# A mixture-of-experts block on one core: gathered token rows transposed by a transposing DMA instead of TensorE

## The chip, the cores and the metric

One Trainium2 chip, and one of its cores is used. The metric is the device time of one execution in microseconds (us); lower is better. The engines are called PE (TensorE, matmuls), DVE (VectorE), ACT (ScalarE), POOL (GpSimd) and SP (SyncE). SP computes nothing here; it issues DMAs.

## What is computed

The input `x` has 4 batches of 512 tokens of 512 features. Each batch first gets a sparse attention matrix added, and then a feed-forward part runs over the normalised tokens. What matters here is its routed half:

```python
logits = x @ router_w.T                         # 8 experts
topk_w, topk_idx = top_k(softmax(logits), 2)    # 2 experts a token, weights normalised to 1
for each expert e:                              # I = 352 hidden features
    out = silu(x @ gate_w[e]) * (x @ up_w[e]) @ down_w[e]
    acc = acc + combine[:, e] * out
moe = acc + shared expert(x)                    # hidden size 704, for all tokens
return x + moe
```

## The kernel before

Four batches are processed in turn (scores, thresholds, normalisation, the shared expert). All of that is the same in both kernels and ends at about 344 us. Then come the routed blocks, which the change touches.

**Blocks.** The 2048 tokens times 2 experts are sorted by expert and cut into blocks of 128 rows. There are up to 39 blocks (`BLOCKS`); 35 are in use with these inputs. For each block j the normalised rows are fetched from DRAM by an indirect DMA (the gather), multiplied by the weights of one expert, scaled by the router's weight, and added into the output in DRAM by another indirect DMA (the scatter, which accumulates). Each value is kept as two float16 parts, hi and lo, so a gathered row has 2 x 512 float16 elements, and each product takes three matmuls. Most tiles of the routed part have two buffers, and block j uses buffer j % 2. Of the gathered rows `xg` these are `qT` and `kT`, of the transposed rows `xT2` two regions of `xT`.

**The steps of block j, by engine.**

- POOL: `gather(j, p)` (lines 548 to 551) copies 128 row numbers into `gidx` (L549), waits for that copy, and issues the gather into `xg` (L550). `scatter(j, m, p)` (lines 553 to 563) waits for the block's result (`s_y2`) and for the scatter before it to have landed (`d_sc`), copies the row numbers into `sidx` (L561), and issues the scatter (L562).
- PE: `routed_x` (L1022) transposes the gathered rows by 8 transposes into bank 0 (L1030). `routed_up` (L1033) runs 24 matmuls for gate and up (L1044 to L1049). `routed_hT` (L1052) transposes the hidden features by 3 transposes (L1057). `routed_down` (L1060) runs 9 matmuls (L1068 to L1070).
- DVE: `routed_x` (L1422) copies bank 0 to `xT2` (L1427), `routed_hidden` forms the product of gate and up (L1433), `routed_h` the lo part of the hidden features (L1438).
- ACT: the activation of the gate (L798), the hi part of the hidden features (L804), and the scaled result into `y2` (L812), for which it waits until the scatter two blocks earlier has landed.

**Order.** Each engine runs its own program in order, and semaphores tie them together. PE's step j is: hidden transposes of j-1, row transposes of j+1, up j, down j-1. DVE's step j is: lo part of j-1, copy of the transposed rows of j+1, two units of expert weights, product of j. ACT's step j is: hi part of j-1, two units of weights, activation of j, result of j-1. POOL's step j waits until PE has transposed block j+1, issues the gather of block j+3 into the buffer that this frees, and then issues the scatter of block j-1. `run_blocks` (L1469) writes out the first 21 steps, loops to 33, and nests the rest in conditions on the number of blocks in use.

**Expert weights.** Each expert has 7 units: 4 of gate and up (two DMAs of 176 KB) and 3 of down (one DMA of 256 KB). SP loads them in float32 into 4 staging places (L400, in `load_ranked`, which waits until the place is free again), ACT makes the hi part (L610) and DVE the lo part (L1121). The first expert and part of the second are there before block 0, and steps 0 to 20 take two units each. SP's program before the change simply goes through the 8 experts (lines 432 to 436), so each load is issued when its place comes free.

Of the kernel before, what the change touches and what calls it, by code (L numbers as in the profile page):

```python
# [59 lines left out]
HEAD_BLOCKS = 21  # L60
GROUP = 8
# [64 lines left out]
def build(nc, x, ctx_in, wq, wk, gamma, router, gate, up, down, s_gate, s_gate_b, s_up, s_up_b, s_down, s_down_b,  # L126
# [6 lines left out]
    def sem(name):  # L133
        return es.enter_context(nc.semaphore(name))
# [72 lines left out]
    sg2 = sgt[:, :, 0:I]  # L207
    xT2 = xT[:, :, :, :].rearrange("p s c t -> p (s c t)")[:, 0:4 * KD * P].rearrange("p (a s c t) -> p a s c t", a=2, s=2, c=KD)
# [66 lines left out]
    d_xg = [sem(f"d_xg{i}") for i in range(2)]  # L275
    d_sc = [sem(f"d_sc{i}") for i in range(2)]
# [52 lines left out]
    s_x2ps = sem("s_x2ps")  # L329
    s_x2 = sem("s_x2")  # L330
# [16 lines left out]
    def _(sp):  # L347
# [85 lines left out]
        for r in range(E):  # L433
            expert = sp.value_load(order[0:1, r:r + 1].bitcast(I32), min_val=0, max_val=E - 1)
            for n in range(RANKED + r * PER_EXPERT, RANKED + (r + 1) * PER_EXPERT):
                load_ranked(n, expert)
# [6 lines left out]
    def _(pool):  # L443
# [135 lines left out]
        pool.wait_ge(s_x2ps, 1)  # L579
# [3 lines left out]
        def step(j, m, p, fetch=True):  # L583
            if fetch:
                pool.wait_ge(s_x2ps, j + 2)
                gather(j + 3, 1 - p)
            if not (isinstance(j, int) and j == 0):
                scatter(j - 1, m if p else m - 1, 1 - p)
# [244 lines left out]
    def _(pe):  # L833
# [188 lines left out]
        def routed_x(j, m, p):  # L1022
            pe.wait_ge(d_xg[p], 16 * (m + 1))
            if isinstance(j, int) and j == 0:
                pe.wait_ge(s_route, 1)
            else:
                pe.wait_ge(s_x2, j)
            o = bank[0][:, :].bitcast(F16)
            for c in range(2 * KD):
                last = pe.transpose(o[:, c * P:(c + 1) * P], xg[p][:, c * P:(c + 1) * P], ident16[:, :])  # L1030
            last.then_inc(s_x2ps, 1)

        def routed_up(j, p, at):  # L1033
            pe.wait_ge(s_x2, j + 1)
# [41 lines left out]
        def step(j, m, p, fetch=True):  # L1076
            first_block = isinstance(j, int) and j == 0
            if not first_block:
                routed_hT(j - 1, 1 - p)
            if first_block or not (isinstance(j, int) and j == BLOCKS - 1):  # L1080
                routed_x(j + 1, m + (1 if p else 0), 1 - p)
            at = where(j)
            if not isinstance(j, int):
                pe.wait_ge(s_wloD, EARLY + (E - 1) * PER_EXPERT)
            elif j == 0:
                pe.wait_ge(s_wlo, SECOND - EARLY)
            elif j % 4 == 0 and j < HEAD_BLOCKS:
                pe.wait_ge(s_wloD, EARLY + j // 4 * PER_EXPERT)
            routed_up(j, p, at)
            if not first_block:  # L1090
                routed_down(j - 1, 1 - p, where(j - 1))

        routed_x(0, 0, 0)
# [9 lines left out]
    def _(dve):  # L1103
# [318 lines left out]
        def routed_x(j, p):  # L1422

            dve.wait_ge(s_x2ps, j + 1)
            if not (isinstance(j, int) and j < 2):
                dve.wait_ge(s_gu2, j - 1)
            dve.tensor_copy(xT2[:, p, :, :, :].rearrange("p s c t -> p (s c t)").bitcast(F32), bank[0][:, :]).then_inc(s_x2, 1)  # L1427

# [12 lines left out]
        def step(j, m, p, fetch=True):  # L1441
# [3 lines left out]
            if first_block or not (isinstance(j, int) and j == BLOCKS - 1):  # L1445
                routed_x(j + 1, 1 - p)
# [6 lines left out]
        def later_weights(k):  # L1453
            for _ in range(k):
                weight_lo(next(later))

        later_weights(4)
        routed_x(0, 0)
        later_weights(sum(SECOND_AT) - 4)

# [53 lines left out]
```

## Time and profile before

| | us |
|---|---|
| median of 3 runs | 588.96 |
| lowest and highest | 588.16, 589.74 |
| the profiled execution | 589.12 |
| its span | 587.3 |
| mean granted clock of TensorE | 0.906 of full speed |

The span runs from the first to the last instruction; the time of the execution has 1.8 us more around it. In the profile, busy time is the time in which an engine ran instructions; L1030 is line 1030 of the kernel; "x34" is a count. A wait is put down to what released it. PE overlaps the end of one matmul with the next, so the time of one (mean ns) is longer than the distance of two. "SPq" is the queue of SP, in which issues of DMAs are seen. A DMA "lands" when its semaphore says that all its data have arrived; the time to landing counts from its issue.

### The profile page before, as it was taken

Reading aid. Unit: us, or ns where it says so; the run is one execution under the profiler, and the core shown is the slowest. Engines: PE = TensorE matmul, PEld = TensorE weight load, DVE = VectorE, ACT = ScalarE, POOL = GpSimd, SP = SyncE. Lnnn points to the kernel's source line nnn. Section 1 sums busy time; section 2 is a strip of 40 time slices with the busy share of each in tenths; the row PEclk is TensorE's granted clock in tenths of the full one; section 3 lists DMA queues with packets and bytes.
Section 4 is the critical chain, followed back from the end, with each engine's and each line's share of the span. In section 5 each row is a group of like instructions: output and inputs, shape, how many; then the busy total and the mean of one; then the engine's idle time right before and its main releaser. Section 6 shows DMA issues by size and latency. Waiting matters only on the chain.

```text
span 587.3 us, 9556 instructions
## 1 busy us (share of the span) xinstructions
PE 478.6 (81%) x2914; PEld 269.9 (46%) x2915; DVE 341.8 (58%) x890; ACT 236.0 (40%) x417; POOL 196.2 (33%) x247
## 2 busy tenths in 40 slices
PE   5220539979799869976898989999999999999970
PEld 2000324434343434433445546666666666666640
DVE  1699787688677976785299365545545533223210
ACT  3552265443654374443443244444444432222220
POOL 0012245004300070004219433544454454544531
PEclk9765769999699988998699799999999999999985
DMA  5701240004700162005333295677688745454451
GB/s 139 247 18 36 90 144 19 1 0 128 179 1 1 71 133 83 1 1 145 73 99 104 86 266 174 158 208 188 163 199 181 171 74 94 83 89 90 75 91 18
DMA packets 36926, 60.51 MB, mean 103 GB/s; under 512 B 6153, under 2 KB 16649, under 8 KB 36882
## 3 DMA queue, kind: packets, MB, share of 16 engines
q0 software_dynamic: 10384, 23.34, 21.9%
q1 hardware_dynamic: 26498, 36.60, 19.6%
q8 instruction: 25, 0.41, 0.3%
q14 instruction: 19, 0.16, 0.1%
HBM read 37.64 MB, written 22.28 MB: 102 GB/s over the span
## 4 chain that ended last, share of the span: by engine, by line
PE 61%; DVE 20%; ACT 6%; issue 6%; DMA 3%; POOL 3%; DVEq 0%; SPq 0%; ACTq 0%; POOLq 0%
PE bank L925 5%; PE bank L926 5%; PE bank L927 5%; PE bank L1068 4%; PE bank L1070 4%; PE bank L1069 4%; PE bank L1044 4%; PE bank L1048 3%; PE bank L1046 3%; PE bank L1047 3%; PE bank L1049 3%; PE bank L1045 3%; PE bank L1030 3%; PE bank L871 2%; PE bank L1057 2%
## 5 line engine op out<-in xcount | busy, mean ns | idle before, releaser
L925 PE MATMUL bank<-xT,W 128*128 128x512 f16 x176 | 69.8, 397 | 0.0
L926 PE MATMUL bank<-xT,W 128*128 128x512 f16 x176 | 69.8, 396 | 0.0
L927 PE MATMUL bank<-xT,W 128*128 128x512 f16 x176 | 69.5, 395 | 0.0
L562 POOL DMA_INDIRECT out_dram<-xb,sidx x35 | 56.8, 1624 | 29.7 <-POOL sidx L561 28.6
L1438 DVE TENSOR_TENSOR hS<-bank,hS 128x384 f16<-128x384 f32 x35 | 19.5, 558 | 73.4 <-ACT hS L804 67.3
L798 ACT ACTIVATE sgt<-bank 128x352 f32<-128x352 f32 x35 | 16.2, 463 | 86.2 <-PE bank L1049 86.2
L1433 DVE SCALAR_TENSOR_TENSOR xb<-bank,sgt 128x352 f32<-128x352 f32 x35 | 18.4, 525 | 54.7 <-ACT sgt L798 54.7
L492 POOL TENSOR_TENSOR rstd<-pw 128x4 f32<-128x4 f32 x12 | 12.5, 1042 | 107.4 <-DVE pw L1149 107.1
L812 ACT ACTIVATE xb<-bank,wcol 128x512 f32<-128x512 f32 x35 | 24.1, 688 | 56.8 <-PE bank L1070 55.3
L937 PE MATMUL bank<-W,hS 128*128 128x512 f16 x96 | 37.1, 387 | 10.8 <-DVE hS L1303 9.4
L1044 PE MATMUL bank<-W,xT 128*128 x140 | 43.8, 313 | 0.2 <-issue 0.2
L1046 PE MATMUL bank<-W,xT 128*128 x140 | 43.8, 313 | 0.0
L1049 PE MATMUL bank<-W,xT 128*128 x140 | 43.8, 313 | 0.0
L1047 PE MATMUL bank<-W,xT 128*128 x140 | 43.8, 313 | 0.0
L1045 PE MATMUL bank<-W,xT 128*128 x140 | 43.8, 313 | 0.0
L1048 PE MATMUL bank<-W,xT 128*128 x140 | 43.8, 313 | 0.0
L662 ACT ACTIVATE sgt<-bank,bias 128x512 f32<-128x512 f32 (+1 forms) x24 | 16.5, 687 | 66.0 <-PE bank L927 66.0
L1068 PE MATMUL bank<-W,hS 128*128 x105 | 40.5, 386 | 1.3 <-DVE hS L1438 1.3
L1069 PE MATMUL bank<-W,hS 128*128 x105 | 40.6, 386 | 0.0
L1070 PE MATMUL bank<-W,hS 128*128 x105 | 40.6, 386 | 0.0
L938 PE MATMUL bank<-W,hS 128*128 128x512 f16 x96 | 36.9, 384 | 0.0
L939 PE MATMUL bank<-W,hS 128*128 128x512 f16 x96 | 36.9, 384 | 0.0
(230 smaller groups left out, 1082.5 us busy)
## 6 DMA issues: line engine op xcount, KB each, us to landing
xn_dram<-xn SPq DMA_DIRECT2D x17, 256.0 KB, 2.0
xb<-x_in SPq DMA_DIRECT2D x4, 1024.0 KB, 6.4
out_dram<-xb SPq DMA_DIRECT2D x16, 256.0 KB, 2.6
out_dram<-ysh POOLq DMA_DIRECT2D x12, 256.0 KB, 4.1
stage<-L_ffn_down_w_in SPq DMA_DIRECT2D x12, 256.0 KB
sim<-L_ffn_down_w_in SPq DMA_DIRECT2D x12, 256.0 KB
stage<-L_ffn_gate_w_in SPq DMA_DIRECT2D x16, 176.0 KB
stage<-L_ffn_up_w_in SPq DMA_DIRECT2D x16, 176.0 KB
```

What stands on the lines that cost most here:

```text
L925: pe.matmul(o, wh, xT[:, 0, c, :], start=(c == 0), stop=False)
L926: pe.matmul(o, wh, xT[:, 1, c, :], start=False, stop=False)
L927: last = pe.matmul(o, wl, xT[:, 0, c, :], start=False, stop=(c == KD - 1))
L1044: pe.matmul(og, xh, W[:, bass.ds(hi, I)], start=f, stop=False)
L1045: pe.matmul(ou, xh, W[:, bass.ds(hi + I, I)], start=f, stop=False)
L1046: pe.matmul(og, xh, W[:, bass.ds(lo, I)], start=False, stop=False)
L1047: pe.matmul(ou, xh, W[:, bass.ds(lo + I, I)], start=False, stop=False)
L1048: pe.matmul(og, xl, W[:, bass.ds(hi, I)], start=False, stop=z)
L1049: last = pe.matmul(ou, xl, W[:, bass.ds(hi + I, I)], start=False, stop=z)
L1068: pe.matmul(o, hh, wh, start=(c == 0), stop=False)
L1069: pe.matmul(o, hh, wl, start=False, stop=False)
L1070: last = pe.matmul(o, hl, wh, start=False, stop=(c == DC - 1))
```

## The change

PE's eight transposes a block and DVE's copy go. In their place SP issues one transposing DMA a block, from `xg` to `xT2`, which turns the 128 rows of 1024 float16 elements into 8 tiles of 128 x 128. `xT2` and the new view `xt2` are the same memory. SP issues it for block j+2 in its step j, after the wait for the gather (`d_xg`) and for the up matmuls of block j (`s_gu2`), which read the same buffer. PE's up part of block j waits for the landing (`d_xt`) instead of DVE's copy. POOL's gather of block j+3 waits for the landing of the transposing DMA of block j+1 instead of PE's transposes. SP has one program for both: the loads of weights are now cut into portions, 11 units ahead of the first transposing DMA, 7 behind the second, and then two units in each of the steps 0 to 18, ahead of that step's transposing DMA.

```diff
--- before.py
+++ after.py
@@ -58,6 +58,7 @@
 BLOCKS = T * TOPK // P + E - 1
 SURE = 33
 HEAD_BLOCKS = 21
+LOADING = 19
 GROUP = 8
 TABLE_AT = {3: (0, 8), 4: (8, 16), 5: (16, 2 * NT)}
 PLACES = 4
@@ -205,6 +206,7 @@
     y2 = xb[:, 0:2, :]
     h2 = xb[:, 2:4, 0:I]
     sg2 = sgt[:, :, 0:I]
+    xt2 = xT[:, :, :, :].rearrange("p s c t -> p (s c t)")[:, 0:4 * KD * P].rearrange("p (a n t) -> p a n t", a=2, n=2 * KD)
     xT2 = xT[:, :, :, :].rearrange("p s c t -> p (s c t)")[:, 0:4 * KD * P].rearrange("p (a s c t) -> p a s c t", a=2, s=2, c=KD)
     hT2 = hS[:, :, 0:DC, 0:2 * P].rearrange("p s c (a t) -> p s c a t", a=2)
     rt = sigA[:, :, :].rearrange("p a b -> p (a b)")
@@ -273,6 +275,7 @@
     d_y = [sem(f"d_y{i}") for i in range(2)]
     d_stage = [sem(f"d_stage{i}") for i in range(PLACES)]
     d_xg = [sem(f"d_xg{i}") for i in range(2)]
+    d_xt = [sem(f"d_xt{i}") for i in range(2)]
     d_sc = [sem(f"d_sc{i}") for i in range(2)]
     s_const = sem("s_const")
     s_zero = sem("s_zero")
@@ -326,8 +329,6 @@
     s_oneh = sem("s_oneh")
     s_tabp = sem("s_tabp")
     s_route = sem("s_route")
-    s_x2ps = sem("s_x2ps")
-    s_x2 = sem("s_x2")
     s_gu2 = sem("s_gu2")
     s_sig2 = sem("s_sig2")
     s_h2 = sem("s_h2")
@@ -430,10 +431,45 @@
             if b + 1 < NB:
                 sp.dma_start(xb[:, :, :], x[b + 1].rearrange("(t p) d -> p t d", p=P)).then_inc(d_x, 16)
         sp.wait_ge(s_order, 1)
-        for r in range(E):
-            expert = sp.value_load(order[0:1, r:r + 1].bitcast(I32), min_val=0, max_val=E - 1)
-            for n in range(RANKED + r * PER_EXPERT, RANKED + (r + 1) * PER_EXPERT):
-                load_ranked(n, expert)
+        ranked = iter(range(RANKED, len(UNITS)))
+        expert = [None]
+
+        def load_more(k):
+
+            for _ in range(k):
+                n = next(ranked)
+                if (n - RANKED) % PER_EXPERT == 0:
+                    r = (n - RANKED) // PER_EXPERT
+                    expert[0] = sp.value_load(order[0:1, r:r + 1].bitcast(I32), min_val=0, max_val=E - 1)
+                load_ranked(n, expert[0])
+
+        def routed_x(j, m, p):
+
+            sp.wait_ge(d_xg[p], 16 * (m + 1))
+            if not (isinstance(j, int) and j < 2):
+                sp.wait_ge(s_gu2, j - 1)
+            sp.dma_start_transpose(xt2[:, p, :, :], xg[p][:, :]).then_inc(d_xt[p], 16)
+
+        load_more(PER_EXPERT + PLACES)
+        sp.wait_ge(s_route, 1)
+        sp.wait_ge(s_gu, NB * SC)
+        routed_x(0, 0, 0)
+        routed_x(1, 0, 1)
+        load_more(sum(SECOND_AT))
+
+        def step(j, m, p, fetch=True):
+            if isinstance(j, int) and j < LOADING:
+                load_more(BLOCK_UNITS)
+            if not (isinstance(j, int) and j + 2 >= BLOCKS):
+                routed_x(j + 2, m + 1, p)
+
+        def finish(j):
+            for i in range(2):
+                sp.wait_ge(d_xt[i], 16 * ((min(j + 2, BLOCKS - 1) + 2 - i) // 2))
+
+        for j in range(SURE):
+            step(j, j // 2, j % 2)
+        rest(sp, sp.value_load(used, min_val=0, max_val=BLOCKS), SURE, step, finish)
         sp.wait_ge(d_x1, 16 * NT)
         for i in range(2):
             sp.wait_ge(d_xn[i], 16 * NT // 2)
@@ -576,13 +612,13 @@
         gather(1, 1)
         for t in range(TB - 1):
             add_shared(NB - 1, t, ylasts[t])
-        pool.wait_ge(s_x2ps, 1)
+        pool.wait_ge(d_xt[0], 16)
         gather(2, 0)
         add_shared(NB - 1, TB - 1, ylasts[TB - 1])
 
         def step(j, m, p, fetch=True):
             if fetch:
-                pool.wait_ge(s_x2ps, j + 2)
+                pool.wait_ge(d_xt[1 - p], 16 * (m + 1 + p))
                 gather(j + 3, 1 - p)
             if not (isinstance(j, int) and j == 0):
                 scatter(j - 1, m if p else m - 1, 1 - p)
@@ -1019,19 +1055,10 @@
         shared_down_pair(NB - 1)
         shared_down(NB - 1, 2)
 
-        def routed_x(j, m, p):
-            pe.wait_ge(d_xg[p], 16 * (m + 1))
+        def routed_up(j, m, p, at):
+            pe.wait_ge(d_xt[p], 16 * (m + 1))
             if isinstance(j, int) and j == 0:
                 pe.wait_ge(s_route, 1)
-            else:
-                pe.wait_ge(s_x2, j)
-            o = bank[0][:, :].bitcast(F16)
-            for c in range(2 * KD):
-                last = pe.transpose(o[:, c * P:(c + 1) * P], xg[p][:, c * P:(c + 1) * P], ident16[:, :])
-            last.then_inc(s_x2ps, 1)
-
-        def routed_up(j, p, at):
-            pe.wait_ge(s_x2, j + 1)
             if not (isinstance(j, int) and j < 2):
                 pe.wait_ge(s_h2, j - 1)
             else:
@@ -1077,8 +1104,6 @@
             first_block = isinstance(j, int) and j == 0
             if not first_block:
                 routed_hT(j - 1, 1 - p)
-            if first_block or not (isinstance(j, int) and j == BLOCKS - 1):
-                routed_x(j + 1, m + (1 if p else 0), 1 - p)
             at = where(j)
             if not isinstance(j, int):
                 pe.wait_ge(s_wloD, EARLY + (E - 1) * PER_EXPERT)
@@ -1086,11 +1111,10 @@
                 pe.wait_ge(s_wlo, SECOND - EARLY)
             elif j % 4 == 0 and j < HEAD_BLOCKS:
                 pe.wait_ge(s_wloD, EARLY + j // 4 * PER_EXPERT)
-            routed_up(j, p, at)
+            routed_up(j, m, p, at)
             if not first_block:
                 routed_down(j - 1, 1 - p, where(j - 1))
 
-        routed_x(0, 0, 0)
         shared_down(NB - 1, TB - 1)
 
         def finish(j):
@@ -1419,13 +1443,6 @@
         dve.tensor_scalar(wcol[:, :], tab[:, 1, :], 1.0 / HW, None, ALU.mult)
         dve.scalar_tensor_tensor(idx[:, :], tab[:, 0, :], -1.0, zer, ALU.add, ALU.add).then_inc(s_route, 1)
 
-        def routed_x(j, p):
-
-            dve.wait_ge(s_x2ps, j + 1)
-            if not (isinstance(j, int) and j < 2):
-                dve.wait_ge(s_gu2, j - 1)
-            dve.tensor_copy(xT2[:, p, :, :, :].rearrange("p s c t -> p (s c t)").bitcast(F32), bank[0][:, :]).then_inc(s_x2, 1)
-
         def routed_hidden(j, p):
             dve.wait_ge(s_sig2, j + 1)
             if not (isinstance(j, int) and j < 2):
@@ -1442,8 +1459,6 @@
             first_block = isinstance(j, int) and j == 0
             if not first_block:
                 routed_h(j - 1, 1 - p)
-            if first_block or not (isinstance(j, int) and j == BLOCKS - 1):
-                routed_x(j + 1, 1 - p)
             if isinstance(j, int) and j < HEAD_BLOCKS:
                 later_weights(BLOCK_UNITS)
             routed_hidden(j, p)
@@ -1454,9 +1469,7 @@
             for _ in range(k):
                 weight_lo(next(later))
 
-        later_weights(4)
-        routed_x(0, 0)
-        later_weights(sum(SECOND_AT) - 4)
+        later_weights(sum(SECOND_AT))
 
         def finish(j):
             routed_h(j, j % 2)
```

## Rows read from the trace of the kernel before

**Rows 1.** The page: span, and busy time, share and instructions of PE; the chain by engine.

```profile
span 587.3 us, 9556 instructions
PE 478.6 (81%) x2914; PEld 269.9 (46%) x2915; DVE 341.8 (58%) x890; ACT 236.0 (40%) x417; POOL 196.2 (33%) x247
...
PE 61%; DVE 20%; ACT 6%; issue 6%; DMA 3%; POOL 3%; DVEq 0%; SPq 0%; ACTq 0%; POOLq 0%
```

**Rows 2.** The table of windows (from:to, length, then as headed).

```profile
core 0: us, PE busy (x) PEld busy (x) DVE busy (x) ACT busy (x) POOL busy (x), PEclk, DMA share, GB/s
...
334.00:338.00 4.00, 4.00 (x21) 1.79 (x19) 1.02 (x2) 2.33 (x5) 1.01 (x1) 1.00 0.23 70
...
450.00:470.00 20.00, 20.00 (x140) 12.73 (x138) 10.02 (x18) 8.81 (x16) 9.19 (x13) 1.00 0.76 183
...
480.00:500.00 20.00, 20.00 (x142) 12.84 (x140) 5.04 (x9) 4.59 (x9) 9.23 (x14) 1.00 0.52 97
```

**Rows 3.** The chain of waits in order of time, two blocks (start, us, what).

```profile
357.80 0.33 PE bank L1057 x3
358.13 0.45 PE bank L1030 x8
...
458.73 0.33 PE bank L1057 x3
```

**Rows 4.** Groups by line, 351 to 567 us (busy us, mean ns | idle before).

```profile
L1427 DVE COPY xT<-bank 128x512 f32<-128x512 f32 x34 | 23.1, 681 | 0.0
...
L1030 PE MATMUL bank<-ident,kT 128*128 128x128 f16 x136 | 10.4, 219 | 0.0
L1030 PE MATMUL bank<-ident,qT 128*128 128x128 f16 x136 | 10.4, 219 | 0.0
```

**Rows 5.** What POOL waited for, 391 to 477 us (us in total, times, longest).

```profile
POOL sidx L561 <- DMA out_dram<-xb,sidx: 23.5, 13, 2.4
```

**Rows 6.** POOL's timeline (start, us, instruction, idle before it): scatters and one gather.

```profile
359.75 1.65 POOL L562 DMA_INDIRECT out_dram<-xb,sidx  x1 [0.88 <-POOL sidx L561]
...
391.11 1.61 POOL L562 DMA_INDIRECT out_dram<-xb,sidx  x1 [0.84 <-POOL sidx L561]
...
445.23 1.60 POOL L562 DMA_INDIRECT out_dram<-xb,sidx  x1 [0.84 <-POOL sidx L561]
446.27 0.77 POOL L549 COPY gidx<-idx 128x1 int32<-128x1 int32 x1
447.83 1.01 POOL L550 DMA_INDIRECT qT<-xn_dram,gidx  x1 [0.79 <-POOL gidx L549]
450.11 0.19 POOL L561 COPY sidx<-idx 128x1 int32<-128x1 int32 x1 [1.28 <-DMA out_dram<-xb,sidx]
451.13 1.61 POOL L562 DMA_INDIRECT out_dram<-xb,sidx  x1 [0.84 <-POOL sidx L561]
...
476.44 1.61 POOL L562 DMA_INDIRECT out_dram<-xb,sidx  x1 [0.84 <-POOL sidx L561]
...
517.99 1.60 POOL L562 DMA_INDIRECT out_dram<-xb,sidx  x1 [0.84 <-POOL sidx L561]
...
575.63 1.59 POOL L562 DMA_INDIRECT out_dram<-xb,sidx  x1 [0.85 <-POOL sidx L561]
```

**Rows 7.** Landing of the scatters (L562), issued in 351 to 400 and in 480 to 588.

```profile
DMA to landing us min/median/max: 5.0/5.1/6.3
...
DMA to landing us min/median/max: 4.6/4.8/5.1
```

**Rows 8.** DMA issues of the page (count, KB each, median us to landing).

```profile
xn_dram<-xn SPq DMA_DIRECT2D x17, 256.0 KB, 2.0
...
kT<-ctx_in SPq DMA_DIRECT2D x4, 256.0 KB, 5.1
...
hS<-L_ffn_s_up_w_in SPq DMA_DIRECT2D x4, 32.0 KB, 4.2
```

**Rows 9.** SP's timeline: a load of expert weights before block 0.

```profile
337.89 0.33 SPq L400 DMA_DIRECT2D sim<-L_ffn_down_w_in  x1
```

**Rows 10.** The chain of waits, the end of the last block.

```profile
566.14 1.87 issue
...
570.40 0.43 PE bank L1069
570.82 0.43 PE bank L1070
```

## The prediction, made before the changed kernel was run

> **What bounds the kernel now.** I began with the page: the span is 587.3 us and PE, busy for 478.6 us of it, has 61% of the chain that ended last [rows 1]. The change touches only the routed blocks, so the rest of the reading is in their stretch. The table of windows shows PE busy all the time there, at a granted clock of 1.00 (the upper of its two levels, 2.4 GHz), with the DMA engines at 0.76 while expert weights are loading and at 0.52 afterwards [rows 2]. The chain of waits in order of time gives the beat: the transposes of L1057 begin at 357.80 and again at 458.73, 16 blocks later, which is 6.31 us a block, and the eight transposes of the gathered rows (L1030) take 0.45 us of each [rows 3]. So on PE alone the change looks like 0.45 us a block.
>
> The next view is what POOL waits for. Between 391 and 477 us, 13 times, the scatter's index copy (L561) is released by the landing of the scatter before it, not by the result of the block [rows 5]. Scatters accumulate into the output and so go one at a time: L562 issued at 445.23 lands shortly before 450.11, the index is copied, and the next one is issued at 451.13 [rows 6]. From landing to next issue it is 1.02 us, the same everywhere. This is a second chain beside PE's, and its beat is what I count on:
> - scatters 5 to 18, while weights load: 391.11 to 476.44, 13 intervals, 6.56 us each [rows 6], longer than PE's 6.31;
> - scatters 18 to 25, after the loads: 476.44 to 517.99, 7 intervals, 5.94 us each [rows 6].
> PE does not feel the 6.56 today: a scatter may run late by some microseconds before ACT's copy of a later block (L812, which waits for the scatter two before) holds up PE. In the first stretch the scatter chain falls behind by 13 x 0.25 = 3.3 us, in the second it catches up.
>
> **The change part by part.** Call the transposing DMA T.
> - PE loses 8 transposes a block: 34 blocks x 0.45 = 15.3 us (block 0's are under the start, below) [rows 3, 4]. PE's beat would be 5.85 us.
> - DVE loses the copy of L1427, 0.68 us a block [rows 4]. Worth nothing: DVE is idle for about half of these windows [rows 2] and PE never waits for this copy. Nothing is late in its place.
> - The scatter chain keeps everything that it has. With PE at 5.85, it is the longer one in every stretch. I sum its 34 intervals: the first 5 had landings of median 5.1 [rows 7], so 6.12 each, 30.6; 13 at 6.56, 85.3; 16 at 5.94, 95.0; together 210.9 us. Before, the first and last scatter are 575.63 - 359.75 = 215.9 us apart [rows 6]. That is 5.0 us less, not 15.3, and the first scatter comes 0.45 us earlier: 5.4 us in all, if T disturbs nothing.
> - T adds 256 KB to the DMA engines for each block, in the flight of one scatter. No row shows a T. The nearest price: with the expert loads (two units a block, 2176 KB an expert over 3.5 blocks, 622 KB a block) the scatter interval is 6.56 instead of 5.94, 0.62 us for 622 KB. By bytes T costs 0.62 x 256/622 = 0.26 us an interval. The lower end is 0: a T that falls between two flights; below nothing is excluded, as T takes no traffic away. The upper end goes by rows: T has 1024 pieces of 256 B, the loads have 402 rows a block, 0.62 x 1024/402 = 1.6 us. I take 0.26, as source, size and queue are nearest to a plain transfer of 256 KB: 34 x 0.26 = 8.8 us.
> - T's own latency: a plain 256 KB store from this memory lands in 2.0 us, a 256 KB load in 512 B rows in 5.1, and 32 KB in 256 B rows in 4.2 [rows 8]. So T is between 2.0 and 8 x 4.2 = 34 us; I take 5.1, the nearest in size and row. It is issued when the up matmuls of block j end (wait on s_gu2) and needed when those of j+2 begin, 2 x 5.85 less the 3.5 us of one up part, 8.2 us later: hidden.
> - The gather now waits for T's landing instead of PE's transposes, and POOL's scatter is queued behind that gather. Gather and its index take POOL from 446.27 to 448.84, and 1.27 us are then free before the next landing at 450.11 [rows 6]. T(j+1) lands well before scatter j-1 can go (that needs up j and down j-1 as well), so I cost this at nothing; if T were late, every us beyond 1.27 would go into the scatter's interval.
> - Round of a buffer: T, then the gather of two blocks later (index, 0.8 us, issue and landing; the landing isn't shown, the scatter's 5.0 bounds it: 6.0 in all), then T again. Two blocks give 11.7 us, so T may take 5.7.
> - SP: an issue of a plain 128-row load holds it 0.33 us [rows 9]. T holds it for at least that and, if it goes with the pieces, 8 x 0.33 = 2.7 us; with four loads' 1.4 us that is 4.1 of 5.85. The loads of block j+1 are queued behind T(j+2)'s waits, but their place comes free only in DVE's step j+1, later than the end of up j. Nothing.
> - Start: T(0) and T(1) stand ahead of the load issued at 337.89 [rows 9], on which the first block's path hangs. Gathers are issued by 333.4, and the DMA engines are only 0.23 busy in 334 to 338 [rows 2], so both fit there. Between 0 and two landings of 5.1 us less the gap; I take 0. PE's 0.45 for block 0 is hidden too, since block 0 ends in a wait for weights.
> Sum against the profiled execution: 589.1 - 5.4 + 8.8 = 592.5 us; it was 0.2 above the median of the runs, so 592.3. (Of the 589.1, 1.8 us lie outside the span; I leave them as they are.)
>
> On the price of T's issue a page speaks against the change. The Trainium skill, page DMA: Bandwidth & Descriptors, calls the crossbar's work a 256-byte tile transpose (section SDMA does more than copy), and its table of sequencer times gives, for the generation before the third, 262,144 cycles for 8,192 tiles of an SBUF to SBUF transpose. By that, taken literally and scaled by a plain DMA's 512 cycles to the 0.33 us seen here, 1024 tiles would hold SP for an estimated 21 us. The page's own limits (16 rows by 128 elements is the smallest tile, section DMA Transpose) make it 64 tiles and 1.3 us. No run so far shows either.
>
> **The rivals.**
> A. The scatter chain sets the beat, but T doesn't stretch it: 583.7 - 0.2 = 583.5, faster. For: in the late windows the DMA engines are half idle, and PE's slack lets T move to where there is room. Against: the chain has a scatter in flight 4.9 of 5.94 us, so T nearly always meets one. It decides at 0.16 us a scatter, where 34 x 0.16 eats the 5.4.
> B. All of PE's gain arrives: 589.1 - 15.3 - 0.2 = 573.6. It needs scatter intervals under 5.85, landings under 4.83. Late landings go down to 4.6, but the median there is 4.8 and with loads 5.1 and above [rows 7], with more traffic to come.
> C. The round of a buffer becomes the bound. From a landing of T of 5.7 us on, each us more costs half a us a block. At 8.2 us (the geometric mean of 2.0 and 34) a block takes (8.2 + 6.0)/2 = 7.1 us: 34 x 7.1 - 210.9 = 30.5 more than A, 614. For: small pieces are slow, 4.2 us for 32 KB [rows 8]. PE then idles 1.2 us a block; after an idle of 1.87 us the matmuls of the last block come 0.43 us apart, not 0.22, the lower of the two clock levels [rows 10], so a part of this may double. PE's blocks would then be far longer.
> D. T holds SP, and so the loads and the next T: the beat is T's hold plus 1.4 us of loads. It decides from 4.4 us of hold on. 8 issues give 2.7; at double that, 5.4, the beat is 6.8 us, and the time 583.5 + 34 x 6.8 - 210.9 = 604. By the page's literal tile count, above, it would be far over 1000.
> E. No change, 589: POOL's chain and PE's already pace each other, and what PE saves turns into a wait of PE. Against: the sum of the intervals is 5 us shorter than what is measured between first and last scatter.
>
> **How the numbers follow.** Forecast (scatter chain stretched by T) 0.50, with its own range 587 to 605 (0.1 to 0.63 us a scatter); A 0.20; B 0.07; C 0.13; D 0.04; E 0.06. About 0.3% is what a measurement of this kernel can tell from no change: 587.2 to 590.7. Faster: A, B and 0.02 of the forecast, 0.29. The same: E and 0.09 of the forecast (stretches of 0.11 to 0.21), 0.15. Slower: the rest, 0.56. The range 581 to 622 leaves out B, D's literal case and the upper half of C, with the top end of the stretch, 0.18 together.
>
> **What would show it.** Right: L1030 and L1427 are gone; in 390 to 560 us L561 is released by the scatter's landing nearly every time; scatter intervals of about 6.8 us with loads and 6.2 after; PE shows waits of some tenths a block, at ACT's or T's results. T lands in about 5 us and SP is held under 3. Wrong: PE without waits and 5.85 us a block (B); intervals as before (A); up matmuls released by T, with T over 5.7 us (C); SP's issues back to back (D). The forecast falls if the scatter's landings don't grow, or if something other than the scatter chain paces the late blocks.

## The result, and the profile after

| | before | after |
|---|---|---|
| median, us | 588.98 | 607.25 |
| lowest and highest | 588.16, 589.74 | 604.12, 611.76 |
| the profiled execution | 589.12 | 611.76 |
| its span | 587.3 | 609.9 |
| mean granted clock of TensorE | 0.906 | 0.891 |

The change makes the kernel slower: 1.030 times the time before (95% interval 1.025 to 1.036). The forecast was 592.3 us, slower, in a range of 581 to 622. The executions of the changed kernel spread over 7.6 us, those of before over 1.6 (on other chips, 11 to 13 of them, over 3.3 to 7.4). The profiled one is the slowest of the four, so its own sums below come out some microseconds above the median.

The page of the changed kernel, read as [rows 1]: span, engines, packets, one DMA queue, and the chain by engine and by line.

```profile
span 609.9 us, 8961 instructions
PE 472.0 (77%) x2626; PEld 255.5 (42%) x2627; DVE 321.7 (53%) x854; ACT 236.1 (39%) x417; POOL 197.6 (32%) x247
...
DMA packets 75997, 70.18 MB, mean 115 GB/s; under 512 B 45226, under 2 KB 55722, under 8 KB 75955
...
q1 hardware_dynamic: 65570, 46.31, 29.8%
...
DMA 35%; PE 24%; DVE 20%; issue 8%; ACT 6%; POOL 4%; SPq 0%; POOLq 0%; DVEq 0%; ACTq 0%
DMA out_dram<-xb,sidx 32%; PE bank L961 4%; PE bank L963 4%; PE bank L962 4%; PE bank L907 2%; DVE hS L1327 2%; POOL xn L539 2%; DVE stats L1168 2%; DVE top L1248 2%; DVE sgt L1338 1%; DMA sim<-L_ffn_up_w_in 1%; POOL sidx L597 1%; PE bank L973 1%; ACT xT L724 1%; PE bank L975 1%
```

PE had 61% of the chain that ended last [rows 1] and now has 24%. The scatter (`out_dram<-xb,sidx`), which was no item of that line before, has 32%: it is the routed part. PE has fewer instructions and idles more.

The same two lines of the page of the kernel before:

```profile
DMA packets 36926, 60.51 MB, mean 103 GB/s; under 512 B 6153, under 2 KB 16649, under 8 KB 36882
...
q1 hardware_dynamic: 26498, 36.60, 19.6%
```

The 37 transposing DMAs bring 39,072 packets more in queue q1, 1056 each, and 39,073 more under 512 B: 256 KB in pieces of 256 B make 1024 of the 1056, and 32 more come with them. The queue's time rises from 0.196 x 587.3 = 115 us of all 16 engines to 0.298 x 609.9 = 182, so one transposing DMA takes 1.8 us of all 16.

What was waited for in the stretch after the loads (490 to 560 us), and a window in it, as in [rows 2] (from:to, length, then PE, PEld, DVE, ACT and POOL busy, clock, DMA share, GB/s):

```profile
ACT xb L848 <- DMA out_dram<-xb,sidx: 34.8, 11, 4.4
POOL sidx L597 <- DMA out_dram<-xb,sidx: 23.0, 11, 2.5
...
PEld bank L1071 <- issue: 7.9, 10, 1.9
...
510.00:530.00 20.00, 18.41 (x112) 10.99 (x111) 3.25 (x6) 4.41 (x9) 8.80 (x12) 1.00 0.68 115
```

The kernel before, in the same stretch and the same window:

```profile
POOL sidx L561 <- DMA out_dram<-xb,sidx: 8.2, 6, 1.6
POOL sidx L561 <- ACT xb L812: 8.0, 5, 1.8
...
510.00:530.00 20.00, 20.00 (x144) 12.88 (x142) 5.45 (x10) 5.36 (x11) 9.19 (x13) 1.00 0.48 92
```

All 11 scatters of this stretch are now released by the landing of the one before; in the kernel before it was 6 of 11, and the block's result (L812) released the others. ACT too now waits for landings ahead of its copy of the result (L848), which it did not do here before, and hands PE the wait. The DMA share is 0.68 where it was 0.48.

The timeline of one block and its neighbour there (POOL and SP), against [rows 6]:

```profile
506.66 1.01 POOL L586 DMA_INDIRECT kT<-xn_dram,gidx  x1 [0.79 <-POOL gidx L585]
...
509.83 0.18 POOL L597 COPY sidx<-idx 128x1 int32 x1 [2.16 <-DMA out_dram<-xb,sidx]
...
510.85 1.23 SPq L451 DMA_TRANSPOSE xT<-kT  x1
510.85 1.60 POOL L598 DMA_INDIRECT out_dram<-xb,sidx  x1 [0.84 <-POOL sidx L597]
...
516.46 0.18 POOL L597 COPY sidx<-idx 128x1 int32 x1 [2.00 <-DMA out_dram<-xb,sidx]
517.49 1.61 POOL L598 DMA_INDIRECT out_dram<-xb,sidx  x1 [0.85 <-POOL sidx L597]
```

From one issue to the next it is 6.64 us, with the same 1.02 us from the start of the copy, which the landing releases, to the issue. The row to look at is the pair at 510.85. The gather is issued 2.6 us after a scatter, lands 4.2 us later, and that landing releases SP's transposing DMA, at the moment at which the next scatter is issued. From 504 us to the end, each transposing DMA is issued within 0.4 us of a scatter, as the gather that releases it always stands 2.6 us behind a scatter in POOL's program: the two fly together in every one of these blocks.

Landings of the scatters (L598) issued in 395 to 480 and in 480 to 590, against [rows 7], and of the transposing DMAs (L451) over the whole kernel, with SP's time for one (the form with qT):

```profile
DMA to landing us min/median/max: 4.8/5.5/6.8
...
DMA to landing us min/median/max: 5.0/5.6/6.1
...
L451 SPq DMA_TRANSPOSE xT<-qT x19: 1232/1240/2243, 334.5 to 585.5; - x19
...
DMA to landing us min/median/max: 3.0/4.7/8.4
```

Summed as in the prediction, for the two profiled executions (each interval is the time from one scatter's issue to the next):

| | before | forecast | after |
|---|---|---|---|
| first scatter issued at | 359.75 | 359.3 | 363.27 |
| 5 first intervals, mean | 6.27 | 6.38 | 7.61 |
| 13 with loads | 6.56 | 6.82 | 6.90 |
| 16 after | 6.20 | 6.20 | 6.69 |
| first to last scatter | 215.9 | 219.7 | 234.9 |

### The profile page after: what moved, and what is told of

The parts are those of the page before. It is cut to its first block, busy times and chain, and to the rows that moved or that the text cites. A ratio compares the mean times of both kernels' runs of the same rounds, so it can differ in the third digit from the quotient of the medians.

```text
span 609.9 us, 8961 instructions
## 1 busy us (share of the span) xinstructions
PE 472.0 (77%) x2626; PEld 255.5 (42%) x2627; DVE 321.7 (53%) x854; ACT 236.1 (39%) x417; POOL 197.6 (32%) x247
## 3 DMA queue, kind: packets, MB, share of 16 engines
q1 hardware_dynamic: 65570, 46.31, 29.8%
## 4 chain that ended last, share of the span: by engine, by line
DMA 35%; PE 24%; DVE 20%; issue 8%; ACT 6%; POOL 4%; SPq 0%; POOLq 0%; DVEq 0%; ACTq 0%
DMA out_dram<-xb,sidx 32%; PE bank L961 4%; PE bank L963 4%; PE bank L962 4%; PE bank L907 2%; DVE hS L1327 2%; POOL xn L539 2%; DVE stats L1168 2%; DVE top L1248 2%; DVE sgt L1338 1%; DMA sim<-L_ffn_up_w_in 1%; POOL sidx L597 1%; PE bank L973 1%; ACT xT L724 1%; PE bank L975 1%
## 5 line engine op out<-in xcount | busy, mean ns | idle before, releaser
L598 POOL DMA_INDIRECT out_dram<-xb,sidx x35 | 57.0, 1627 | 29.7 <-POOL sidx L597 28.6
L1071 PE MATMUL bank<-W,xT 128*128 x140 | 44.9, 321 | 20.6 <-DMA xT<-kT 12.4
L848 ACT ACTIVATE xb<-bank,wcol 128x512 f32<-128x512 f32 x35 | 24.1, 687 | 89.7 <-DMA out_dram<-xb,sidx 64.2
L1072 PE MATMUL bank<-W,xT 128*128 x140 | 44.7, 319 | 0.0
L1073 PE MATMUL bank<-W,xT 128*128 x140 | 44.7, 319 | 0.0
L1074 PE MATMUL bank<-W,xT 128*128 x140 | 44.6, 319 | 0.0
L1075 PE MATMUL bank<-W,xT 128*128 x140 | 44.5, 318 | 0.0
L1076 PE MATMUL bank<-W,xT 128*128 x140 | 44.5, 318 | 0.0
```

Source lines behind the costliest of these rows:

```text
L598: pool.indirect_dma_start(out=out, out_offset=bass.IndirectOffsetOnAxis(ap=sidx[:, p:p + 1], axis=0), in_=y2[:, p, :], in_offset=None, com ...
L1071: pe.matmul(og, xh, W[:, bass.ds(hi, I)], start=f, stop=False)
L1072: pe.matmul(ou, xh, W[:, bass.ds(hi + I, I)], start=f, stop=False)
L1073: pe.matmul(og, xh, W[:, bass.ds(lo, I)], start=False, stop=False)
L1074: pe.matmul(ou, xh, W[:, bass.ds(lo + I, I)], start=False, stop=False)
L1075: pe.matmul(og, xl, W[:, bass.ds(hi, I)], start=False, stop=z)
```

## The experiments

They ask three things. Is it the serial scatters that set the beat, and not PE waiting for its rows? Does the transposing DMA cost by its bytes or by its pieces? And can the chain be shortened, so that PE's gain arrives? The time of before beside each is that of its own chip, 588.4 to 588.9 us.

### Without the transposing DMA

```diff
-            sp.dma_start_transpose(xt2[:, p, :, :], xg[p][:, :]).then_inc(d_xt[p], 16)
...
-                pool.wait_ge(d_xt[1 - p], 16 * (m + 1 + p))
+                pool.wait_ge(d_xg[1 - p], 16 * (m + 1 + p))
...
-            pe.wait_ge(d_xt[p], 16 * (m + 1))
+            pe.wait_ge(d_xg[p], 16 * (m + 1))
```

> The changed kernel without the transposing DMA: SP issues nothing in its place, PE's up part and POOL's gather wait for the gather of their buffer only (so the up matmuls of the routed blocks read stale rows, and the routed half is wrong). Theory S (the serial scatters set the beat and the transposing DMA stretches each flight): the scatter intervals go back to 5.94 us after the loads and 6.56 with them, PE shows waits of about 0.1 us a block late and 0.7 with loads, and the time is 583.5 us (582 to 586). Rival P (PE's beat of 5.85 us is all that is left once the transfer is gone, and what hurt in the changed kernel was PE waiting for late rows): 573.6 us.

Measured: 582.12 us, ratio 0.991 (0.987 to 0.994). After the loads the scatters are issued 5.8 to 6.1 us apart (one 7.2), 6.03 on average, each released by the landing before it. The waits of POOL, 490 to 560 us, and two scatters:

```profile
POOL sidx L595 <- DMA out_dram<-xb,sidx: 14.3, 11, 1.4
...
508.31 1.61 POOL L596 DMA_INDIRECT out_dram<-xb,sidx  x1 [0.84 <-POOL sidx L595]
514.18 1.60 POOL L596 DMA_INDIRECT out_dram<-xb,sidx  x1 [0.84 <-POOL sidx L595]
```

So PE without its transposes brings 6 us and not 15, since the scatters allow no more: the ceiling of this change, had its DMA been free. In one thing I was off. With the weights loading, the intervals were 6.00 us, not the 6.56 of before, although the same bytes were loaded. How long a scatter flies beside loads is thus not set by their bytes alone; what else sets it is not shown.

### A plain DMA of the same bytes

```diff
-            sp.dma_start_transpose(xt2[:, p, :, :], xg[p][:, :]).then_inc(d_xt[p], 16)
+            sp.dma_start(xt2[:, p, :, :].rearrange("p n t -> p (n t)"), xg[p][:, :]).then_inc(d_xt[p], 16)
```

> The changed kernel with a plain DMA of the same 256 KB from the same source to the same place (128 rows of 2 KB) instead of the transposing one, same waits (the rows are not transposed, so the routed half is wrong). If the price goes by bytes (what I took): nothing changes against the changed kernel, 605 to 609 us, late scatter intervals 6.7. If it goes by pieces: the late intervals fall to 6.0 to 6.2, landings of the scatters to 5.0, the copy lands in under 3 us, and the time is 588 to 594 us.

Measured: 587.03 us (10 runs, 583.6 to 591.5), ratio 0.999 (0.996 to 1.002), just below the 588 to 594 expected by pieces. One late window, POOL's waits and the page's queue:

```profile
490.00:540.00 50.00, 49.90 (x302) 29.86 (x301) 9.21 (x17) 12.63 (x26) 25.07 (x35) 1.00 0.62 133
...
POOL sidx L597 <- DMA out_dram<-xb,sidx: 15.9, 12, 1.6
...
q1 hardware_dynamic: 31826, 46.31, 24.0%
```

The bytes are the same, 46.31 MB in q1, in less than half of the packets: (31,826 - 26,498)/37 = 144 for one copy, against 1056. The copy takes (0.240 x 584.1 - 115)/37 = 0.7 us of all engines, against 1.8 for the transposing one. Late landings of the scatters are 4.8 us at the median (4.5 to 5.0), as before, and the late intervals 5.95. More bytes pass in this window than in the changed kernel (133 GB/s against 114), and the late scatters don't notice. The copy is not free elsewhere: the time is 4.9 us above that without any DMA (582.12), with intervals of 6.21 instead of 6.00 while weights load and the first scatter 2.1 us later. But of the 25 us by which the changed kernel exceeds that run, 20 are gone. A price by bytes is refuted: it is the transposing form of the transfer that costs. This run changes two things at once, the number of packets and the transposing itself; a plain DMA in pieces of 256 B, which would part the two, was not run.

### The kernel before with the transposing DMA beside it

SP's program is that of the changed kernel, but for a few waits that it needs for the idle tile. Everything else is that of before, PE's transposes and DVE's copy too; the DMA moves an idle tile.

```diff
+        def traffic(j, m, p):
+            sp.wait_ge(d_xg[p], 16 * (m + 1))
+            if not (isinstance(j, int) and j < 2):
+                sp.wait_ge(s_gu2, j - 1)
+                sp.wait_ge(d_xt[p], 16 * m)
+            sp.dma_start_transpose(spare_t[:, p, :, :], still[:, :]).then_inc(d_xt[p], 16)
```

> The kernel before, with PE's transposes and DVE's copy, and beside them SP issues the same transposing DMA at the same place as in the changed kernel, but from a tile that nobody writes to one that nobody reads, and nobody waits for it but SP. Theory S: the flights of the scatters grow as in the changed kernel, to 5.6 us late, intervals 6.8 late and 6.9 with loads, and the time is about 604 us (600 to 608). Rival P (the loss comes from PE and POOL waiting for the transposed rows): 589 to 591 us, since nobody waits for these.

Measured: 605.86 us, ratio 1.030 (1.026 to 1.034), which is the changed kernel's own ratio. Landings of the scatters issued in 490 to 560 us, what POOL waited for there, and the transposing DMAs on the page:

```profile
DMA to landing us min/median/max: 5.1/5.5/5.7
...
POOL sidx L603 <- DMA out_dram<-xb,sidx: 22.3, 11, 2.3
...
DMA packets 75999, 70.22 MB, mean 116 GB/s; under 512 B 45225, under 2 KB 55721, under 8 KB 75954
```

Nobody but SP waits for these transfers, and PE does all of its old work. The whole loss is there all the same. So the loss needs no late rows, no round of a buffer, no wait of PE for rows: the traffic on the flights of the scatters is enough. First to last scatter is 233.5 us, the changed kernel's 234.9. That SP now issues the loads in portions is not the cause either: the runs with a plain DMA or none have the same portions, and the worst of them is 4 us above its before.

### The kernel before with a plain DMA beside it

```diff
-            sp.dma_start_transpose(spare_t[:, p, :, :], still[:, :]).then_inc(d_xt[p], 16)
+            sp.dma_start(spare_t[:, p, :, :].rearrange("p n t -> p (n t)"), still[:, :]).then_inc(d_xt[p], 16)
```

> As the kernel before with the idle transposing DMA beside it, but a plain DMA of the same bytes in its place. By bytes: 604 us as there. By pieces: scatter intervals stay under PE's 6.31 us late, and the time is 589 to 593 us.

Measured: 592.58 us, ratio 1.009 (1.006 to 1.013); late landings 4.9 us, against 4.8 before. The same answer from the other side: of 17 us, 13 go with the transposing form, and 4 are left with a plain copy.

### Half of the transposing DMA

```diff
-            sp.dma_start_transpose(xt2[:, p, :, :], xg[p][:, :]).then_inc(d_xt[p], 16)
+            sp.dma_start_transpose(xt2[:, p, 0:4, :], xg[p][:, 0:4 * P]).then_inc(d_xt[p], 16)
```

> The changed kernel with the transposing DMA for the hi half only (512 of the 1024 elements a row, 128 KB in 512 pieces; the lo half of the rows stays stale, so the routed half is wrong). If its price goes by its pieces, half of the 0.84 us that it puts on a late interval is left: 6.36 us late, landings 5.2, time 594 us (591 to 598). If the price is one of its presence (a fixed cost whatever its size): as the changed kernel, 604 to 608.

Measured: 595.77 us, ratio 1.011 (1.006 to 1.016). Scatters after the loads:

```profile
503.58 1.61 POOL L598 DMA_INDIRECT out_dram<-xb,sidx  x1 [0.85 <-POOL sidx L597]
509.78 1.60 POOL L598 DMA_INDIRECT out_dram<-xb,sidx  x1 [0.84 <-POOL sidx L597]
516.16 1.61 POOL L598 DMA_INDIRECT out_dram<-xb,sidx  x1 [0.84 <-POOL sidx L597]
522.26 1.60 POOL L598 DMA_INDIRECT out_dram<-xb,sidx  x1 [0.84 <-POOL sidx L597]
```

Intervals 18 to 33 have a mean of 6.29 us. It is 6.03 without the DMA, 6.73 with all of it. Half of the transfer costs 0.26 us, all of it 0.70: the price grows with the size and is not one of its presence. In time, 582.1, 595.8 and 607.3 us are nearly on a line. The page counts (46,626 - 26,498)/37 = 544 packets for one. Its queue's row reads:

```profile
q1 hardware_dynamic: 46626, 41.46, 24.0%
```

That is (0.240 x 591.0 - 115)/37 = 0.7 us of all engines, no more than the plain copy of twice the bytes, and yet the late scatters feel it and do not feel the copy. So neither bytes nor the engines' time gives the price; the number of packets does in these four runs, with the transposing itself as the rival that no run excludes.

### The index copy ahead of the waits

If the chain is landing, 1.02 us, issue, landing, the 1.02 us can be taken off it. The copy of the row numbers needs neither the result nor the landing.

```diff
+            link2(pool.tensor_copy(sidx[:, p:p + 1], idx[:, bass.ds(j, 1)]), s_si, j + 1)
             if isinstance(j, int) and j == 0:
...
             pool.wait_ge(s_y2, j + 1)
             if not (isinstance(j, int) and j == 0):
                 pool.wait_ge(d_sc[1 - p], 16 * (m + 1) if p else 16 * m)
-            link2(pool.tensor_copy(sidx[:, p:p + 1], idx[:, bass.ds(j, 1)]), s_si, j + 1)
+            pool.sem_inc(s_held, 1)
```

In the changed kernel:

> The changed kernel, but POOL copies a scatter's row numbers (sidx) ahead of its waits for the block's result and for the scatter before, so that the copy is no part of the serial chain. Theory S (the chain is landing, 1.02 us, issue, landing): up to 1.0 us comes off each of 34 intervals; late intervals 5.85 (then PE's beat), with loads 6.1, first five 6.8, sum 207 us instead of 235, time 580 us (575 to 588). Rival Q (the 0.84 us before the issue is the indirect DMA's own preparation on POOL, which the copy doesn't cause, so only 0.2 us comes off): 600 us.

Measured: 601.62 us, ratio 1.018 (1.013 to 1.023). First to last scatter is 228.2 us where it was 234.9. POOL's timeline:

```profile
508.29 1.01 POOL L586 DMA_INDIRECT qT<-xn_dram,gidx  x1 [0.79 <-POOL gidx L585]
509.29 0.21 POOL L591 COPY sidx<-idx 128x1 int32 x1
511.48 1.61 POOL L599 DMA_INDIRECT out_dram<-xb,sidx  x1 [1.98 <-DMA out_dram<-xb,sidx]
...
514.07 1.01 POOL L586 DMA_INDIRECT kT<-xn_dram,gidx  x1 [0.79 <-POOL gidx L585]
515.07 0.20 POOL L591 COPY sidx<-idx 128x1 int32 x1
518.61 1.60 POOL L599 DMA_INDIRECT out_dram<-xb,sidx  x1 [3.34 <-DMA out_dram<-xb,sidx]
```

The copy is out of the chain, and the row names the landing as what releases the scatter. But the issue does not come at the landing. The scatter of 511.48 took this long to land:

```profile
DMA to landing us min/median/max: 6.3/6.3/6.3
```

So it landed at 517.8, and the next was issued at 518.61, 0.8 us later. Over the 34 intervals of this trace landing and next issue are never less than 0.77 us apart, at the median 0.8; with the copy in the chain it was 1.2. That is rival Q: the wait of 0.84 us before a scatter's issue is not the copy's, and moving the copy takes only 0.2 to 0.4 us off. Q's time of 600 us came about for Q's reason. The flights grew a little as well, to a late median of 5.7 us, with landings in 480 to 595 us of up to 7.0, where they reached 6.1 before the move. The mean late interval is 6.53, 0.2 shorter; in the load stretch nothing is won (6.97). Why the flights grew is not shown.

In the kernel before:

> The same move in the kernel before. Its scatter chain doesn't hold up PE, whose beat is 6.31 us: theory S gives no change, 586 to 589 us. If the scatter chain did cost PE something there, it would be faster, about 583 us.

Measured: 586.52 us (10 runs, 585.0 to 589.7), ratio 0.995 (0.992 to 0.999). POOL's timeline, two scatters:

```profile
504.41 1.60 POOL L563 DMA_INDIRECT out_dram<-xb,sidx  x1 [2.48 <-ACT xb L813]
510.73 1.61 POOL L563 DMA_INDIRECT out_dram<-xb,sidx  x1 [2.51 <-ACT xb L813]
```

The intervals are 6.3 us on average, PE's beat, and after the loads nearly every scatter is released by its block's result (L813) instead of by a landing. As expected, PE was not held up. The interval of the ratio lies just below 1, and of the versions that compute the whole output this is the only one whose median came out below both kernels. The profile does not show where 2 us would come from (first to last scatter 215.8 us, before 215.9), so I count it as half a per cent at the edge of what can be measured.

### The transposing DMA ahead of the loads

```diff
-            if isinstance(j, int) and j < LOADING:
-                load_more(BLOCK_UNITS)
             if not (isinstance(j, int) and j + 2 >= BLOCKS):
                 routed_x(j + 2, m + 1, p)
+            if isinstance(j, int) and j < LOADING:
+                load_more(BLOCK_UNITS)
```

> The changed kernel with SP's step turned round: the transposing DMA of block j+2 ahead of the two units of weights instead of behind them. Theory: the first blocks' wait for transposed rows shrinks (first five intervals 6.9 instead of 7.6 us), the late ones stay at 6.75, time 602 to 605 us. Rival: the loads, now behind the wait for the gather, come late, and ACT and DVE wait for weights: 610 us or more.

Measured: 606.18 us, ratio 1.025 (1.017 to 1.032). The time missed the expected 602 to 605. The first five intervals fell from 7.61 to 7.01 us as expected, the others stayed (6.94, 6.71). But with the index copy early and the loads still ahead they take 6.79, so this pair of traces doesn't show that the order did it. Against the 607.25 of the changed kernel, the difference in time is inside the spread of both.

With both moves:

> Both moves in the changed kernel: the index copy ahead of the waits, and the transposing DMA ahead of the loads. Theory S: 3 to 4 us below the run with the index copy alone, about 576 us. If that run is at 600 us (rival Q), this is at 597.

Measured: 601.11 us, ratio 1.019 (1.014 to 1.025), with single runs from 595 to 604. No better than the index copy alone, and above the 597 us expected under rival Q.

### Every other block

PE transposes the odd blocks' rows, the DMA the even blocks'. With the index copy early:

```diff
-            if not (isinstance(j, int) and j + 2 >= BLOCKS):
+            if p == 0 and not (isinstance(j, int) and j + 2 >= BLOCKS):
                 routed_x(j + 2, m + 1, p)
...
+            if p:
+                pe.wait_ge(s_x2, m + 1)
+            else:
+                pe.wait_ge(d_xt[p], 16 * (m + 1))
```

> Even blocks' rows by the transposing DMA, odd blocks' by PE's eight transposes and DVE's copy, with the index copy ahead of the waits. PE's beat is then 6.08 us on average (5.85 and 6.31). Theory S: a scatter that meets a transposing DMA takes 6.0 to 6.5 us from issue to issue, one that doesn't 5.1, 5.8 on average, so PE sets the beat: 588.9 - 34 x 0.23 = 581 us (578 to 585), faster than both kernels. Rival: the flights grow as they did with the index copy alone (late intervals 6.5), and nothing is won: 588 to 592 us.

Measured: 594.69 us, ratio 1.013 (1.009 to 1.017), single runs 586.4 to 599.3. The profiled execution, one of the two fastest (586.8 us), shows this:

```profile
499.22 1.61 POOL L599 DMA_INDIRECT out_dram<-xb,sidx  x1 [1.80 <-DMA out_dram<-xb,sidx]
505.66 1.60 POOL L599 DMA_INDIRECT out_dram<-xb,sidx  x1 [2.65 <-DMA out_dram<-xb,sidx]
511.34 1.61 POOL L599 DMA_INDIRECT out_dram<-xb,sidx  x1 [1.87 <-DMA out_dram<-xb,sidx]
517.74 1.60 POOL L599 DMA_INDIRECT out_dram<-xb,sidx  x1 [2.61 <-DMA out_dram<-xb,sidx]
```

A clean step: 6.44, 5.68, 6.40 us, by turns with and without a transposing DMA in the flight. In these rows one costs 0.7 us; late landings are 5.6 to 5.9 us with it, 4.7 to 5.0 without. But the chain still waits for landings each time, and nothing is won at the median. The expectation of 581 us missed. I had reckoned 5.1 us for an interval without the DMA, and 5.7 is what it took: a flight of 4.9 and the 0.8 us that stay between landing and issue. Why the other executions are up to 12 us longer is not shown by this profile.

The same alternation without the early index copy:

> The same alternation without the move of the index copy: intervals late 5.94 and 6.78 by turns, 6.36 on average, with loads 6.6, first five 6.6: 33 + 86 + 102 = 221 us between first and last scatter, 590 to 594 us, no faster than before.

Measured: 601.42 us, ratio 1.021 (1.015 to 1.027); slower than the 590 to 594 expected. The late intervals go 6.0 and 6.8 by turns, as expected, but in the load stretch some are 8 to 9 us long.

### Neither the DMA nor the copy in the chain

The kernel of the first experiment, with the index copy early.

> No transposing DMA at all (the up matmuls read stale rows, the routed half is wrong) and the index copy ahead of the waits. Neither the serial scatters nor the transfer holds up PE then. Theory S: PE's own beat, 5.85 us in every stretch, and 574 us (572 to 577): all of the 15.3 us that the page of PE promised. Rival: something else (loads, ACT) holds the loading stretch above 5.85, and it stays near 580.

Measured: 580.31 us, ratio 0.984 (0.979 to 0.989). The expected 574 us (572 to 577) missed. The intervals did fall to PE's beat, 5.85 with loads and 5.84 after (without the last one), and PE waits for next to nothing in between. The scatters are mostly still released by landings, 0.8 us after each, so the two chains are about equal here. From first to last scatter it is 205.2 us, 10.7 shorter than before instead of 15.3. The two ends hold back the rest: the first five intervals take 6.46 us and the last one 9.2 (7.7 before). And the first scatter comes at 362.77, 3.0 us later than before. PE's timeline there (first) and in the changed kernel (second), at the end of block 0:

```profile
351.96 0.90 PE L1083 MATMUL bank<-ident,xb 128*128 128x128 f32 x3 [3.61 <-DVE xb L1449]
```

```profile
352.97 0.90 PE L1084 MATMUL bank<-ident,xb 128*128 128x128 f32 x3 [4.80 <-DVE xb L1450]
```

Before, the same wait was 2.65 us and the three transposes took 0.55 at the full clock. Now PE idles 3.6 and 4.8 us and comes back at the lower clock level: 0.90 us, and matmuls of the changed kernel's next block 0.29 us apart instead of 0.15. It is so in all traces: with all of PE's transposes (before and the three runs made from it) the idle time is 2.65 to 2.8 us and the three take 0.55; with the transposes gone or halved it is 2.9 to 6.1 and they take 0.90. PE, sooner at the wait for block 0's weights by its saved transposes, got there only to idle. In the changed kernel the wait also ends later, at 352.97 instead of 351.09. The chain of waits shows a load of weights in it that took 7.4 us to land, where the same load took 5.1 before:

```profile
342.48 7.40 DMA sim<-L_ffn_up_w_in
```

```profile
343.29 5.12 DMA sim<-L_ffn_up_w_in
```

The first two transposing DMAs, issued at 334.48 and 336.42, had landed by then (after 3.6 and 4.8 us), so the load did not queue behind them. What held it is not shown.

## Why the prediction was right, and what it had wrong

- **What bounds.** Right, and the central step: the serial scatters are a second chain, PE's 15.3 us can't arrive, and without disturbance the change is worth about 5 us. The first experiment gave 582.1 for the forecast's 583.5, in part by luck: its intervals with loads were 13 x 0.56 = 7 us shorter than the sum had them, and the first five, the late ones and the start together 5 us longer. The waits shift as said: to landings at POOL in every block, and through ACT to PE.
- **The disturbance.** The step "by bytes T costs 0.26 us an interval" failed. Against the run without it, T puts (234.9 - 207.4)/34 = 0.81 us on an interval, 27 us in all for the 8.8 of the sum. Landings after the loads went from 4.8 to 5.6 us, 0.8 us, half of the bound by pieces (1.6), so the price lies between my two rows. The page's row for q1 and the plain copy, with the same bytes and no effect on the late landings, point to the 1056 small packets; the transposing itself is not excluded. In the late stretch, measured against the forecast's own sum, this is 16 x 0.5 = 8 us.
- **The base of that slope was unsound too.** I read 6.56 minus 5.94 us as the price of 622 KB of loads. The same loads went with 6.00 in the first experiment and at PE's pace, 6.30, with the early index in the kernel before. In the load stretch the forecast sum of 6.82 lies near the measured 6.90 only because the two errors cancel.
- **The start.** "Both fit there, I take 0" failed. The first scatter came 4.0 us after the forecast, and the five first intervals took 7.61 instead of 6.38, 6.1 us in all. Of the 4.0 us, 1.2 are there without any transposing DMA too (the first scatter is at 360.52 in the first experiment, where PE came back at the lower clock level as well); the rest goes with the later end of the wait for block 0's weights, above. Why the first five are so long is open: they take 6.56 without T, and 6.63 to 7.61 in the traces with a T in each block.
- Together: 8 + 1 (with loads) + 6 + 4 = 19 us on 592.5 gives 611.5, for the profiled execution's 611.8. So the direction came out right, but the change costs 18 us where I had forecast 3. The median of 607.25 lies beyond the 587 to 605 that I gave the forecast's own mechanism, and inside the whole range only because that reached on to 622 for rival C, which did not happen. That the stated range holds the result is luck as much as insight.
- **Latency and SP.** Right: landing 4.7 us at the median for the 5.1 taken, 3.2 late. SP is held 1.24 us, between 0.33 and 2.7. By the smallest tile that the Trainium skill gives (DMA: Bandwidth & Descriptors, section DMA Transpose), 16 rows by 128 elements, I had made it 64 tiles and, with that page's table of sequencer times, an estimated 1.3 us; the trace agrees. The literal reading of 1024 tiles and 21 us is refuted, and with it rival D.
- **Rivals.** A is what the kernel would be with a free transfer. B never had room. For C the landing would have had to stay above 5.7 us; it did in the first blocks (median 5.8); later the median is 5.1 and then 3.2. PE waited for rows 12 times, 18.5 us in all. The third experiment shows the whole loss without any such wait.

## What to carry to other kernels

Before giving an engine's work to the DMA engines, look for a serial DMA chain beside it, and read who releases what: the saving of the bound engine ends where that chain begins, and the new transfer lands on the chain. Do not price a transfer by its bytes alone: look at its number of packets, as the page counts them, and measure it beside the chain with an idle copy of it, as in the third experiment. A transfer released by a landing can lock itself onto the flight of the next one in the chain; there the half-empty DMA share of a window says nothing about room. And before taking a step out of a serial chain, look at how long after the landing the next issue comes: what stands between them need not be the step.

## What the runs showed of the hardware

- A transposing DMA of 128 rows of 2 KB inside the core's memory goes as 1056 packets, all under 512 B (a plain copy as 144). It takes 1.8 us of all 16 engines (the plain copy 0.7), holds SP 1.24 us (the plain copy 0.47) and lands in 3.2 us beside a scatter (the plain copy in 2.3), in 5.1 beside loads of weights as well (4.5 to 6.5).
- It lengthens an accumulating scatter of 256 KB that flies with it by 0.7 to 0.8 us after the loads; half of it by 0.3; a plain copy of the same bytes not measurably there. The Trainium skill (Advanced Engine Details and Errata, section X-Bar Transpose) says that such DMAs are as fast as regular ones on this chip. Here they are not, for the scatters beside them (second and third experiments) nor by the engines' time, 1.8 against 0.7 us.
- Between the landing of a scatter and the issue of the next by POOL there are 1.2 us with the copy of 128 row numbers between them, and still 0.8 us with the copy made earlier.
- Freed of all or half of its transposes, PE idled 2.9 to 6.1 us at the end of block 0 instead of 2.65 to 2.8, and came back at the lower clock level; a saving ahead of a wait can cost clock behind it.
